# Weight quantization moved into attention, smaller slabs, buffered softmax division and an earlier second half of an FFN tile

## The reference

```python
# layer 0
x = x + _L0_attn_ref(_layernorm(x), ...)   # 16 heads of 64; scores * decay_mask[h, |q-k|], softmax, V, Wo
x = x + _L0_ffn_ref(_layernorm(x), ...)    # quantize x and W to FP6 in blocks of 32; out = xd @ wd.T + bias
# layer 1
x = x + _L1_attn_ref(_layernorm(x), ...)   # 16 heads; out = LN(x + attn(x)) * gamma + beta
x = x + _L1_ffn_ref(_layernorm(x), ...)    # quantize to FP4 in blocks of 16: gate, up, silu(gate)*up, down

# decay mask of layer 0, per head: sum_n softmax(mix)[h, n] * dp[h, n] ** |q - k|
# weights that are quantized: layer 0 W [1024, 1024]; layer 1 w_gate, w_up [2816, 1024], w_down [1024, 2816]
```

## Time and profile before

| | |
|---|---|
| median of 3 runs | 7442.98 us (7442.42 to 7449.43) |
| the profiled execution | 7452.15 us, span 7450.5 us |
| spans of the 8 cores | 7420.1 to 7450.5 us |
| busy share of the span | DVE 57%, PE 37%, ACT 27%, PEld 12%, POOL 3% |
| chain that ended last | DVE 45%, PE 23%, ACT 13%, issue 9%, DMA 6% |

### The profile page before, as it was taken

How to read it: one execution, slowest core, us unless ns; L and a number is a source line. 1 busy time by engine, 2 the same in 40 slices (tenths; PEclk the granted TensorE clock), 3 DMA queues, 4 the chain that set the end, 5 groups by cost and what they waited for, 6 DMA issues and landing times.

```text
span 7450.5 us, 45458 instructions; the slowest of 8 cores (7420.1 to 7450.5 us)
## 1 busy us (share of the span) xinstructions
PE 2779.6 (37%) x9802; PEld 922.3 (12%) x9802; DVE 4273.6 (57%) x4886; ACT 2042.7 (27%) x2842; POOL 250.2 (3%) x277
## 2 busy tenths in 40 slices
PE   2655555655400111136124134474303333333334
PEld 0211111111100000012001011121001111111111
DVE  3444444444297666538898987702326665656666
ACT  2355555555000000024134044473201111111111
POOL 0000000000000000000000000000000010000100
PEclk9756555555755555558567567786656666666666
DMA  3000000000301000120111111101150000000000
GB/s 74 3 3 3 3 3 3 1 0 1 110 23 26 29 31 26 45 60 33 38 41 39 42 33 35 33 3 43 48 110 6 12 6 12 6 12 10 8 12 6
DMA packets 160049, 191.85 MB, mean 26 GB/s; under 512 B 117427, under 2 KB 117427, under 8 KB 159667
## 3 DMA queue, kind: packets, MB, share of 16 engines
q1 hardware_dynamic: 113684, 144.36, 6.5%
q0 software_dynamic: 46112, 44.58, 3.0%
HBM read 133.35 MB, written 52.95 MB: 25 GB/s over the span
## 4 chain that ended last, share of the span: by engine, by line
DVE 45%; PE 23%; ACT 13%; issue 9%; DMA 6%; SPq 2%; DVEq 1%; POOL 1%; ACTq 0%; POOLq 0%
PE a_po L834 4%; ACT a_ebf L820 4%; PE a_psW L801 3%; PE a_pq L760 3%; DVE f_qs_a L238 3%; DVE a_msk L817 3%; DVE f_pw_a L238 3%; PE f_pd L1272 3%; PE a_po L839 2%; ACT a_ebf L824 2%; PE a_pq L721 2%; SPq L557 2%; DMA f_xt<-xs 1%; DVE f_qs_y L228 1%; DMA xs<-a_xtw 1%
## 5 line engine op out<-in xcount | busy, mean ns | idle before, releaser
L817 DVE TENSOR_TENSOR a_msk<-a_psW,a_emask 128x1024 f32<-128x1024 f32 x512 | 623.9, 1224 | 437.6 <-PE a_psW L805 387.2
L834 PE MATMUL a_po<-a_ebf,a_v_all 128*65 128x512 bf16 x1024 | 507.3, 495 | 770.7 <-ACT a_ebf L820 623.1
L820 ACT ACTIVATE a_ebf<-a_msk 128x1024 bf16<-128x1024 f32 x512 | 541.0, 1057 | 591.3 <-DVE a_msk L817 376.0
L824 ACT ACTIVATE a_ebf<-a_psW 128x1024 bf16<-128x1024 f32 x512 | 512.8, 1022 | 132.9 <-PE a_psW L805 124.7
L839 PE MATMUL a_po<-a_ebf,a_v_all 128*65 128x512 bf16 x1024 | 516.3, 504 | 0.0
L801 PE MATMUL a_psW<-a_qp,a_kp 64*128 64x512 bf16 x1024 | 507.0, 507 | 14.9 <-ACT a_kp L767 14.9
L805 PE MATMUL a_psW<-a_qp,a_kp 64*128 64x512 bf16 x1024 | 507.9, 508 | 0.0
L760 PE MATMUL a_pq<-a_u_fm,a_wqkv 128*128 128x512 bf16 x1024 | 255.1, 416 | 579.2 <-DMA a_wqkv<-a_wkT 452.0
L1070 PE MATMUL f_ptr<-f_eye,f_xqb 128*128 128x128 bf16 x128 | 32.5, 264 | 1000.8 <-DVE f_xqb L340 981.3
L1258 PE MATMUL f_ptr<-f_eye,f_hq_s 128*128 128x128 bf16 x352 | 87.2, 266 | 714.0 <-DVE f_hq_s L264 659.8
L865 DVE TENSOR_TENSOR a_attn<-a_pq,a_asb 64x512 bf16<-64x512 f32 x64 | 43.7, 682 | 434.2 <-PE a_pq L861 289.3
(11 more groups left out here) (198 smaller groups left out, 5783.5 us busy)
## 6 DMA issues: line engine op xcount, KB each, us to landing
xs<-a_xtw SPq DMA_DIRECT2D x32, 512.0 KB, 2.6
f_xt<-xs SPq DMA_DIRECT2D x32, 512.0 KB, 3.8
f_pw_wch<-f_wg SPq DMA_DIRECT2D x22, 512.0 KB, 3.4
f_pw_wch<-f_wu SPq DMA_DIRECT2D x22, 512.0 KB, 3.5
f_pw_wch<-f_wd SPq DMA_DIRECT2D x32, 352.0 KB, 3.0
a_xt<-x SPq DMA_DIRECT2D x16, 512.0 KB, 3.6
a_xtw<-x SPq DMA_DIRECT2D x16, 512.0 KB, 3.4
f_xtw<-xs POOLq DMA_DIRECT2D x16, 512.0 KB, 3.7
```

Of the source, the lines that this page charges most:

```text
L817: p.op("vector", lambda e, m3=m3, p3=p3, e3=e3: e.tensor_tensor(m3, p3, e3, ALU.mult), ins=[kA, kB, "emask0", "emask1"], outs=[f"mskp{par}"])
L820: p.op("scalar", lambda e, esl=esl: e.activation(out=ebf[:, esl], in_=msk[:, esl], func=AF.Exp), ins=[f"mskp{par}"], outs=[ek])
L824: p.op("scalar", lambda e, psx=psx, esl=esl: e.activation(out=ebf[:, esl], in_=psx[:], func=AF.Exp, scale=np.float32(0.125)), ins=[kA, kB] ...
L834: p.op("tensor", lambda e, kc=kc, eo=eo, vb=vb: e.matmul(po0[0:65, :], v_all[:, vb: vb + 65], ebf[:, eo: eo + 512], start=(kc == 0), stop= ...
```

## The change

Four things are changed.

1. The quantization of FFN 0's weight is emitted inside attention 0, in slabs of 256 columns (32 units in place of 8). Three units are emitted in each head pair, between the projections and the decay mask, and the last 8 after attention's output projection.
2. FFN 1's weights are quantized in slabs of 512 and 352 columns (88 and 64 units in place of 44 and 32), 3 units after the projections and 4 after each block, which makes 152 in 8 head pairs.
3. At the end of a block (both layers) ACT copies `pq` and `pq2` from PSUM to a new SBUF tile `dnb`, and DVE multiplies `dnb` by `asb`. Both tiles have two buffers, which alternate from block to block.
4. In FFN 0, back(t) is emitted ahead of front(t+2).

```diff
--- before.py
+++ after.py
@@ -575,11 +575,12 @@
     return d
 
 
-def emit_attn(p, dram, layer, prep=None):
-    def prep_step(n=1):
-        if prep is not None:
+def emit_attn(p, dram, layer, prep=None, prep2=None):
+    def prep_step(n=1, site=3):
+        g = prep2 if (site == 2 and prep2 is not None) else prep
+        if g is not None:
             for _ in range(n):
-                next(prep, None)
+                next(g, None)
 
     nc = p.nc
     x_d, y_d, eye_d = dram["x"], dram["y"], dram["eye"]
@@ -612,7 +613,8 @@
     sq_scr = msk[:, 0:D]
     dsc = p.sb("dsc", [128, 512], F32)
     dbf = p.sb("dbf", [128, 512], BF16)
-    asb = p.sb("asb", [128, 512], F32)
+    asb = [p.sb(f"asb{i}", [128, 512], F32) for i in range(2)]
+    dnb = [p.sb(f"dnb{i}", [128, 512], F32) for i in range(2)]
     sc_mask = ExitStack()
     if layer == 0:
         _oact = p.actx
@@ -768,7 +770,7 @@
                     out=dst[:, sl], in_=psel[:], func=AF.Identity,
                     bias=bsb[:, hp:hp + 1]),
                     ins=[kpsel, bkey], outs=[dks + str(ts4)])
-        prep_step(2)
+        prep_step(3, site=2)
 
         if layer == 0:
             for h2 in range(2):
@@ -854,18 +856,22 @@
                                                   in_=dsc[64:65, 0:512], func=AF.Exp,
                                                   scale=np.float32(-1.0)),
                  ins=["dscA"], outs=["dbfA"])
-            p.op("scalar", lambda e: e.activation(out=asb[0:64, :],
+            p.op("scalar", lambda e, qb=qb: e.activation(out=asb[qb % 2][0:64, :],
                                                   in_=po0[0:64, :],
                                                   func=AF.Identity, bias=np.float32(0.0)),
-                 ins=["po0"], outs=["asbA"])
+                 ins=["po0"], outs=[f"asbA{qb % 2}"])
             p.op("tensor", lambda e: e.matmul(pq[0:64, :], ones[64:65, 0:64],
                                               dbf[64:65, 0:512],
                                               start=True, stop=True),
                  ins=["dbfA", "ones"], outs=["pq"])
-            p.op("vector", lambda e, hp=hp, qsl=qsl: e.tensor_mul(
-                attn[0:64, hp * T: (hp + 1) * T][:, qsl], pq[0:64, :],
-                asb[0:64, :]),
-                ins=["pq", "asbA"], outs=[f"attn:{hp}:0:{qb}"])
+            p.op("scalar", lambda e, qb=qb: e.activation(
+                out=dnb[qb % 2][0:64, :], in_=pq[0:64, :],
+                func=AF.Identity, bias=np.float32(0.0)),
+                ins=["pq"], outs=[f"dnbA{qb % 2}"])
+            p.op("vector", lambda e, hp=hp, qsl=qsl, qb=qb: e.tensor_mul(
+                attn[0:64, hp * T: (hp + 1) * T][:, qsl], dnb[qb % 2][0:64, :],
+                asb[qb % 2][0:64, :]),
+                ins=[f"dnbA{qb % 2}", f"asbA{qb % 2}"], outs=[f"attn:{hp}:0:{qb}"])
             p.op("scalar", lambda e: e.activation(out=dsc[0:1, 0:512],
                                                   in_=po1[64:65, :], func=AF.Ln),
                  ins=["po1"], outs=["dscB"])
@@ -874,19 +880,23 @@
                                                   func=AF.Exp,
                                                   scale=np.float32(-1.0)),
                  ins=["dscB"], outs=["dbfB"])
-            p.op("scalar", lambda e: e.activation(out=asb[64:128, :],
+            p.op("scalar", lambda e, qb=qb: e.activation(out=asb[qb % 2][64:128, :],
                                                   in_=po1[0:64, :],
                                                   func=AF.Identity, bias=np.float32(0.0)),
-                 ins=["po1"], outs=["asbB"])
+                 ins=["po1"], outs=[f"asbB{qb % 2}"])
             p.op("tensor", lambda e: e.matmul(pq2[64:128, :], ones[0:1, 0:64],
                                               dbf[0:1, 0:512],
                                               start=True, stop=True),
                  ins=["dbfB", "ones"], outs=["pq2"])
-            p.op("vector", lambda e, hp=hp, qsl=qsl: e.tensor_mul(
-                attn[64:128, hp * T: (hp + 1) * T][:, qsl], pq2[64:128, :],
-                asb[64:128, :]),
-                ins=["pq2", "asbB"], outs=[f"attn:{hp}:1:{qb}"])
-            prep_step(3)
+            p.op("scalar", lambda e, qb=qb: e.activation(
+                out=dnb[qb % 2][64:128, :], in_=pq2[64:128, :],
+                func=AF.Identity, bias=np.float32(0.0)),
+                ins=["pq2"], outs=[f"dnbB{qb % 2}"])
+            p.op("vector", lambda e, hp=hp, qsl=qsl, qb=qb: e.tensor_mul(
+                attn[64:128, hp * T: (hp + 1) * T][:, qsl],
+                dnb[qb % 2][64:128, :], asb[qb % 2][64:128, :]),
+                ins=[f"dnbB{qb % 2}", f"asbB{qb % 2}"], outs=[f"attn:{hp}:1:{qb}"])
+            prep_step(4)
 
     attn_all = [f"attn:{g}:{h2}:{qb}" for g in range(NHP) for h2 in range(2)
                 for qb in range(4)]
@@ -1103,9 +1113,9 @@
     front(0)
     front(1)
     for t in range(NT):
+        back(t)
         if t + 2 < NT:
             front(t + 2)
-        back(t)
 
 
 def build_ffn0():
@@ -1347,19 +1357,26 @@
     dD = declare_ffn1_dram(nc, "f1_", x3, y, eye_d)
     with ctx:
         p = Prog(nc, ctx)
-        with ExitStack() as actx:
-            p.pre, p.actx = "a0_", actx
-            emit_attn(p, dA, 0)
-            p.barrier()
+        with ExitStack() as prepctx0:
+            p.pre, p.actx = "f0p_", prepctx0
+            bufs0 = alloc_prep_bufs(p, slab=256, nm="p0_")
+            gen0 = gen_wprep(p, dB["w"], dB["stg"], *bufs0, 6, NC, D, 256,
+                             tag="f0_")
+            with ExitStack() as actx:
+                p.pre, p.actx = "a0_", actx
+                emit_attn(p, dA, 0, prep2=gen0)
+                for _ in gen0:
+                    pass
+                p.barrier()
         with ExitStack() as actx:
             p.pre, p.actx = "f0_", actx
-            emit_ffn0(p, dB)
+            emit_ffn0(p, dB, prep_done=True)
             p.barrier()
         with ExitStack() as prepctx:
             p.pre, p.actx = "f1_", prepctx
-            scrW, wchW, wqbW = alloc_prep_bufs(p, slab=1024)
+            scrW, wchW, wqbW = alloc_prep_bufs(p, slab=512)
             gen = itertools.chain(*f1_prep_gens(p, dD, scrW, wchW, wqbW,
-                                                slab_gu=1024, slab_d=704))
+                                                slab_gu=512, slab_d=352))
             with ExitStack() as actx:
                 p.pre, p.actx = "a1_", actx
                 emit_attn(p, dC, 1, prep=gen)
```

## The result

The changed kernel takes 7613.88 us (median of 8 runs, 7605.16 to 7625.07), against 7446.21 us before (8 runs). The ratio is 1.0221 (95% interval 1.0209 to 1.0234): 2.2% slower. The prediction was 7620 us, in the range 7540 to 7690.

What follows compares the result with a forecast made beforehand. No engine bounds attention 0, DVE bounds most of attention 1. The terms 149 - 163 + 49 + 142 + 0 = +177 us on the profiled 7452 us give 7629, median 7620 us; range 7540 to 7690.

Steps and rivals of the forecast that it cites:

- The cost by width: DVE units: 0.0150 us per column plus 4.0 us fixed per FP4 unit; 13.3 us per FP6 unit of 256 columns.
- Part 1: +149 and -163: Attention 0: units delay 8 head pairs by 18.6 us each, +149 us; FFN 0's weight behind it shrinks to 106 us, -163.
- Part 3: +49: Attention 0: copies on ACT delay each of 32 blocks by 1.53 us, +49 us; two buffers bring nothing there.
- Part 2: +142: Attention 1: the split adds 304 us of DVE work, waits for copies add 157; attention ends 142 us later.
- Part 4: 0: FFN 0: DVE's waits for matmuls and for the load of x both remain, 0 us, with 15 either way.
- A: Rival: small units cost less than the line says; with all time going with width, -245 us, 7198 us; chance 0.05.
- B: Rival: the wait at head pair boundaries in attention 1 vanishes as weights come in time, 157 us less, 7463; chance 0.04.
- C: Rival: the units in attention 0 hide wholly, 149 us less, 7471; chance 0.04.

Runs made afterwards that it cites:

- e3: The kernel before with part 1 alone, FFN 0's weight in 32 units of 256 columns, 3 per head pair of attention 0: 7424.04 us, ratio 0.9979.
- e2: The kernel before with part 3 alone, two copies per block and two buffers, units as before: 7479.82 us, ratio 1.0061.
- e8: Kernel before, FFN 0's weight between mask products, full-width FFN 1 units spread evenly, early weight loads, copies and two buffers only in layer 1, part 4: 6848.22 us.
- e9: e8 without the copies and with one buffer in both layers: 6863.95 us, ratio 0.9218 to the kernel before.
- e5: The changed kernel with weight loads of head pair hp+2 issued right behind the projections of pair hp: 7468.75 us, ratio 1.0042 to the kernel before.
- e4: The kernel before with part 2 alone, units of 512 and 352 columns in attention 1, one buffer, no copies: 7578.63 us, ratio 1.019.
- e1: The kernel before with part 4 alone, back(t) ahead of front(t+2) in FFN 0: 7448.0 us, ratio 1.0015.
- e7: The kernel before with FFN 0's weight in 16 units of 512 columns, two DVE instructions behind every second mask product of attention 0: 7175.67 us, ratio 0.9644.

## Why the prediction was right

**The cost by width held.** It was drawn from two widths, and the instructions at three new widths (512, 352 and 256 columns) fell within 2 ns of it. For the FP6 unit the gaps between instructions were slightly smaller than I carried over: 12.95 us and not 13.3. This term decided the sign: with the fixed part at zero the forecast would have been 7198.

**Part 1: +149 and -163 were +143 and -165.** The boundary came 17.6 us later for seven head pairs and about 20 for the first, where I had used 18.6 for all. Moving 24 of 32 units gained 22 us by these rows, 16 in e3.

**Part 3: +49 was +50 less 9.** The price per block was 1.56 us for 1.53. The 16 steps of a block were 0.3 us shorter, for a reason that is not known. e2 adds what the prediction did not see: where no unit stands behind the second multiplication, a boundary pays less. In the changed kernel one does stand there. The prediction also found no sign that a multiplication gets 65 ns cheaper when it reads SBUF. It looked at the instruction's own time, which is indeed 0.68 to 0.69 us either way. In e8 against e9, where DVE never waits, two multiplications cost 0.12 us less in a block, 0.06 us each, in the time between instructions. In the changed kernel DVE waits for the copies, and nothing of this can show.

**Part 2: +142 was +134.** The work was 307 us more for 304. The waits were 130.9 + 16.7 = 148 us for 157, and 3 us are the last store, which the table leaves out. Half of what the waits fell short lies at the first boundary, 12.5 us and not 17. There POOL issued both loads at once (3647.57 and 3648.46), and from the next boundary on the second one 5 to 7 us behind the first. The code has the reason: the two loads of a set share one semaphore, and `Prog` raises the wait for the buffer's earlier load to the newest count, which includes the load issued just before. At a buffer's first use there is no earlier load. This stood in the trace of before (3672.98 and 3673.88, then 3960.88 and 3966.41), and I left it out. e5 shows the cause of the waits, e4 shows that the buffers play no part.

**Part 4: 0 was about +4, by its structure.** I had counted one round more and the end shorter and set both to nothing; a round costs 13 us more than a `front` alone, and only 8.8 come back. The measured means over eight cores are +2 us here and +7 in e1.

**The rivals.** A fell on the rows of the new widths. B named the right lever: e5 is rival B made true, and it gave 145 of the 157 us that I had put on it (133 by the ratios). C is false for what was done (e3) and true for a finer grain (e7). The sum was right to 6 us of the median, and part of that is luck. Down the table the errors are -13, -4, -2, +6, -8 and +11 us, which add up to -10 on the profiled execution, and the median lay 5 us under that execution and not 9. The +11 us behind attention 1 are not explained; over the eight cores that stretch is 2363 to 2371 us before and 2365 to 2381 after.

## What to carry to other kernels

Cutting a vector workload into pieces to fit it into gaps is paid with the fixed part of every instruction; take the instruction's time at two widths from the trace first, and compare the sum of the new pieces with the idle time that they are to fill. In an engine with an ordered list a gap is worth only what stands in front of the instruction that waits: 269 us of whole units gained 16 us in gaps of 21 us, and 265 us in gaps of 1.65 us, filled two instructions at a time. A prefetch with two buffers helps nothing when its DMA is queued on an engine behind the stores of the work that it should overlap; a second buffer for a result is worth nothing before that is mended, and here, with its copies, 7 us of 6850 after it.

## What the runs showed of the hardware that was not expected

The instructions laid between the steps of attention 0's chain cost nothing that shows, where they end before DVE's own wait for PE does. With 0.8 to 1.4 us of DVE work put into each of 256 gaps, attention 0 took 1624 us in e7 and 1617 in e8 (1628 before), at a mean granted clock of 0.58 in e7's window, as before.

Dense DVE work beside PE and ACT did not slow them. In e8's attention 1 DVE was busy for 1248 of 1362 us. PE was busy for 683 us there and ACT for 709, against 689 and 711 in the 1824 us of the changed kernel. The granted clock was 0.75 against 0.68.

An fp32 multiplication of 64 x 512 on DVE that read PSUM took the same 0.68 to 0.69 us as one that read SBUF, but it began 0.1 us later behind the instruction ahead of it (e9 against e8). In e9 it also had a second engine to wait for, so the operand's place is not shown to be the cause.
